# A conditioned feed-forward kernel: the aggregation of its channel mixes taken from TensorE to VectorE and GpSimd

## Chip, core and metric

One Trainium2 (trn2) chip, one core of it. The metric is the device time of one execution in microseconds (us), lower is better. Engines: PE is TensorE, DVE is VectorE, ACT is ScalarE, POOL is GpSimd, SP is SyncE, which here only issues DMAs.

## What is computed

For 64 samples, x is 32 channels by 512 features, and a condition vector of 128 numbers belongs to each sample.

```python
h   = gelu(cond @ W0 + b0); h = gelu(h @ W1 + b1)
att = softmax(h @ W2 + b2)                        # 64 x 8
agg_w = einsum('bk,koi->boi', att, weight)        # a 32 x 32 mix for each sample
agg_b = att @ bias_k                              # 64 x 32
hs    = einsum('boi,bih->boh', agg_w, x) + agg_b[:, :, None]
logits = hs @ gate_w;  r = sum(top_2(logits))
shared = relu(hs @ up_w)**2 @ down_w              # 512 -> 1024 -> 512
routed = ((hs @ fc1_w) @ expert_w * r) @ fc2_w    # 512 -> 256 -> 256 -> 512
out = x + layernorm(shared + routed) * gamma + beta
```

All inputs and the output are float32.

## The kernel before, in words

The 64 samples make 16 tiles of 128 rows (4 samples of 32 channels), and the tiles make 4 blocks of 4. Each large product is done as three products of parts, high times high, high times low and low times high (`three_products`, L773 to L776), where the high part is the value rounded to float32r, which ACT writes with a copy, and the low part is the rest, which DVE writes with a subtraction: `up_hi`/`up_lo` (L416, L542), `h_hi`/`h_lo` (L425, L561), `down_hi`/`down_lo` (L478, L664), `sq_hi`/`sq_lo` (both DVE, L589 and L591).

**Head.** PE computes the small network (L725, L728, L732, L733) between filler products that write a bank nobody reads (`stay_warm`, L714). The softmax is spread over ACT and DVE (L410 to L516). The attention is transposed (L740), split (L520, L522), and multiplied with the split kernel tensor in eight products (L746), which leaves every sample's 32 x 32 mix in a PSUM bank. Sixteen small copies of 32 x 32 (L433 on ACT, L569 on DVE) put block 0's mixes on the diagonal of `mix`; sixteen of 32 x 128 (L446, L586) later put all of them into `agg`, from which POOL builds `mix` for the next blocks (`next_mix`, L366). The bias rows come from a product of ones with split products of attention and bias (L527 to L535, L755). `fold_expert` (L719) makes expert_w times fc2_w in plain float32; of its eight calls two stand in the head, one after the mix products of block 0, and five after the first four up chunks.

**Blocks.** Each block does on PE: mix (L760, `mix_chunk`), up (`up_chunk`, eight column groups of four chunks), latent and gate products, then mix of the next block, then down. In block 0 the up products run chunk by chunk over four column groups at once (`up_first_block`, L783), since h arrives chunk by chunk, and then four groups in turn, each of which waits until ACT has emptied its bank (`relu_done`).

**Orders that matter here.** Every engine works through its instructions in the order written. `late` is one buffer of 16 KB a partition: it first takes the raw up weights, then the raw down weights, then x plus beta (`x_beta`) and the output tiles. So SP issues the down loads (L315) only after all of up has been split (L312, L313). POOL's order is: constants, `fc1_lo` (L351), the low gate part (L354), then for block 0 `x_plus_beta` (L371), which waits until two quarters of down have been split (L381, L382), then `next_mix`. SP loads the next block's x into `x_cur` (L319 to L321) only after `xbeta_ready`, since x_plus_beta reads the old x. PE waits for that load at L903, ahead of the next block's mix products.

ACT's order in block 0 is: relu and square of group 0 and 1, each followed by `q_high` (L420), of groups 2 to 5, each followed by a quarter of `down_high`, then 6 and 7. DVE follows with the same pattern (`split_square`, `q_low`, `down_low`). `relu_square` of group m waits for `sq_lo` of group m-2 (L455).

Of the kernel before, what the change touches and what calls it, by code (L numbers as in the profile page):

```python
# [5 lines left out]
def adaln_ffn_kernel(  # L6
# [37 lines left out]
    SR = kernels.shape[0]  # L44
    FIRST, LAST = slice(0, K), slice(SR - K, SR)
# [11 lines left out]
    ONE_BITS = 0x3F800000  # L57
    GC = 96
    WB = 4
    UPC = INT // 4  # L60
# [7 lines left out]
    MIX0_BANK = [7, 4, 7, 4]  # L68
# [7 lines left out]
    experts_v = experts.rearrange("(k p) n -> p k n", p=P)  # L76
    aggb_dram = nc.dram_tensor("aggb_dram", (NB * C,), fp32).ap()

    ctx = ExitStack()
    with ctx:  # L80
# [3 lines left out]
        def sem(name):  # L84
            return ctx.enter_context(nc.semaphore(name))
# [58 lines left out]
        kernels_sb = sb("kernels_sb", [SR, kernels.shape[1]])  # L144
        weight_raw = kernels_sb[:, 0:C * C]
        bias_raw = kernels_sb[:, C * C:C * C + C]
        b2_sb = kernels_sb[0:1, C * C + C:C * C + C + K]
# [3 lines left out]

        att = relu_sq[0:NB, 0, 0:SR]
        att_T = relu_sq[0:2 * K, 1, 0:NB]

        att_parts = sq_hi[0:SR, C * C // TOK, 0:NB]
        weight_parts = sq_hi[0:SR, 0:C * C // TOK, :].rearrange("k a n -> k (a n)")
        bias_parts = sq_lo[0:2 * K, 0, :]
# [3 lines left out]
        att_bias = y_buf[0:2 * K, 0, 0:TOK]  # L161
# [4 lines left out]
        ones = sq_lo[0:2 * K, 1, 0:P]  # L166
# [6 lines left out]
        LOGIT = ps[0:NB, 4, 192:192 + K]  # L173
        ATT_T = ps[0:SR, 4, 256:256 + NB]
        IDLE = ps[0:GC, 0, 0:2 * GC]
        AGG_B = ps[:, 1, :]
        AGGB_ROWS = ps[0:NB, 3, 0:C]
# [3 lines left out]

        AGG = ps[:, 5, :].rearrange("p (c b) -> p c b", b=NB)

        def agg_src(q, g, tiles):

            return AGG[q * C:(q + 1) * C, :, g:tiles * G:G]

        def agg_part(g, q):
            return agg[g * C:(g + 1) * C, :, q:C:G].rearrange("i n c -> i c n")

        def mix_part(g, q):
            return mix[g * C:(g + 1) * C, :, g * C + q:(g + 1) * C:G].rearrange("i t c -> i c t")
# [13 lines left out]
        kernels_loaded = sem("kernels_loaded")  # L206
        experts_loaded = sem("experts_loaded")
        x_loaded = sem("x_loaded")
        up_loaded = [sem(f"up_loaded{i}") for i in range(4)]
# [19 lines left out]
        att_hi_ready = sem("att_hi_ready")  # L229
        att_lo_ready = sem("att_lo_ready")  # L230
        weight_hi_ready = sem("weight_hi_ready")
        weight_lo_ready = sem("weight_lo_ready")
        attb_hi_ready = sem("attb_hi_ready")
        attb_lo_ready = sem("attb_lo_ready")
        agg_done = sem("agg_done")
# [12 lines left out]
        agg_act = sem("agg_act")  # L248
        agg_dve = sem("agg_dve")
        up_hi_ready = sem("up_hi_ready")  # L250
        up_lo_ready = sem("up_lo_ready")
        fc1_hi_ready = sem("fc1_hi_ready")
# [44 lines left out]
        def _(sp):  # L297
            sp.dma_start(mlp_sb[:, :], mlp).then_inc(mlp_loaded, 16)
            sp.dma_start(kernels_sb[:, :], kernels).then_inc(kernels_loaded, 16)
            sp.dma_start(experts_sb[:, :, :], experts_v).then_inc(experts_loaded, 16)  # L300
            sp.dma_start(x_cur[:, :, :], x_v[:, 0:TB, :]).then_inc(x_loaded, 16)
            for i in range(4):
                sp.dma_start(up_raw[:, :, i * UPC:(i + 1) * UPC],
                             up_v[:, :, i * UPC:(i + 1) * UPC]).then_inc(up_loaded[i], 16)

# [6 lines left out]
            sp.wait_ge(up_hi_ready, 4)  # L312
            sp.wait_ge(up_lo_ready, IC)  # L313
# [28 lines left out]
        def _(pool):  # L342
# [6 lines left out]
            nc.gpsimd.memset(half[:, :], -0.5).then_inc(const_ready, 1)  # L349
            pool.wait_ge(fc1_hi_ready, 1)  # L350
# [5 lines left out]
            pool.wait_ge(agg_act, 2 * G)  # L356
            pool.wait_ge(agg_dve, 2 * G)
# [38 lines left out]
        def _(act):  # L396

            act.wait_ge(dve_const, 1)
# [570 lines left out]
```

## Time and profile before

| | |
|---|---|
| runs of the kernel | 268.87 us median of 3 (268.6 to 269.01) |
| profiled execution, span from the first to the last instruction | 266.2 us |
| busy share of the span | PE 97%, DVE 58%, ACT 32%, POOL 17% |
| instructions | 3377 |

The profile is that of one execution; its own time is not given apart from its span, and the median of the runs is 2.7 us above the span. A row of a timeline or chain gives the start and the duration in us, the engine and the line. A row of a group of instructions gives their count, then their busy time and the mean duration in ns of one, then the idle time of the engine just before them and what ended it. PEld is PE's weight load.

### The profile page before, as it was taken

The page shows a single profiled execution, that of the slowest core. Times are in us where ns is not written, and L with a number is a line of the kernel's source. Part 1 is how long each engine was busy: PE and PEld are TensorE (multiplying, and loading weights), DVE is VectorE, ACT ScalarE, POOL GpSimd, SP SyncE. Part 2 cuts the span into 40 slices and gives each one's busy share as a digit, 9 for nine tenths or more (in the row PEclk, how much of TensorE's full clock was granted, in tenths as well). Part 3 has the DMA queues.
Part 4 walks back from the last instruction along what each step waited for, and adds up shares of the span by engine and source line. Part 5 has one row for each costly group of instructions (what it writes and reads, how often), then busy time and mean ns, then how long its engine had stood idle before and what let it go on. Part 6 is the DMA issues. An engine that isn't in the chain of part 4 may idle for free.

```text
span 266.2 us, 3377 instructions
## 1 busy us (share of the span) xinstructions
PE 259.0 (97%) x1222; PEld 215.7 (81%) x1222; DVE 154.9 (58%) x268; ACT 85.2 (32%) x146; POOL 44.6 (17%) x42
## 2 busy tenths in 40 slices
PE   7999999999999999999999999999999999999991
PEld 7698888788888888888888888888888888778891
DVE  3686899974444954384544963384444963314454
ACT  4356994441111354241110354231110355211110
POOL 1000409101111800001111810001111700001111
PEclk9999999999999999999999999999999999999997
DMA  6973710400111240000111140000111100001111
GB/s 211 342 224 147 264 52 10 151 0 0 42 39 39 49 151 0 0 0 4 39 39 39 42 155 0 0 0 0 39 39 39 42 0 0 0 2 39 39 39 39
DMA packets 9132, 15.71 MB, mean 59 GB/s; under 512 B 634, under 2 KB 3578, under 8 KB 9122
## 3 DMA queue, kind: packets, MB, share of 16 engines
q1 hardware_dynamic: 9122, 15.57, 17.4%
q8 instruction: 7, 0.11, 0.2%
q14 instruction: 3, 0.02, 0.0%
HBM read 11.37 MB, written 4.20 MB: 58 GB/s over the span
## 4 chain that ended last, share of the span: by engine, by line
PE 95%; issue 2%; DVE 1%; POOLq 0%; POOL 0%; DVEq 0%
PE ps L774 26%; PE ps L776 26%; PE ps L775 26%; PE ps L760 6%; PE ps L714 2%; PE ps L719 2%; PE ps L838 1%; PE ps L840 1%; PE ps L746 1%; PE ps L850 1%; POOLq L80 0%; POOL rstd L378 0%; PE ps L755 0%; DVE stats L617 0%; DVE y_buf L615 0%
## 5 line engine op out<-in xcount | busy, mean ns | idle before, releaser
L774 PE MATMUL ps<-down_hi,sq_hi 128*128 128x512 f32 (+1 forms) x136 | 51.3, 377 | 0.0
L775 PE MATMUL ps<-down_lo,sq_hi 128*128 128x512 f32 (+1 forms) x136 | 51.2, 377 | 0.0
L776 PE MATMUL ps<-down_hi,sq_lo 128*128 128x512 f32 (+1 forms) x136 | 51.2, 377 | 0.0
L774 PE MATMUL ps<-h_hi,up_hi 128*128 128x512 f32 x128 | 50.3, 393 | 0.0
L776 PE MATMUL ps<-h_hi,up_lo 128*128 128x512 f32 x128 | 49.8, 389 | 0.0
L775 PE MATMUL ps<-h_lo,up_hi 128*128 128x512 f32 x128 | 49.8, 389 | 0.0
L378 POOL TENSOR_TENSOR rstd<-mv,half 128x1 f32<-128x1 f32 x16 | 15.7, 982 | 177.4 <-DVE mv L622 171.9
L456 ACT ACTIVATE relu_sq<-ps 128x512 f32<-128x512 f32 x32 | 19.1, 597 | 58.1 <-PE ps L776 44.2
L615 DVE TENSOR_TENSOR y_buf<-ps,y_buf 128x512 f32<-128x512 f32 x15 | 10.4, 691 | 45.9 <-PE ps L776 45.9
L589 DVE CAST sq_hi<-relu_sq 128x512 fp32r<-128x512 f32 x32 | 23.6, 737 | 20.9 <-ACT relu_sq L458 20.2
L473 ACT ACTIVATE y_buf<-ps,top 128x512 f32<-128x512 f32 x16 | 11.0, 689 | 69.2 <-PE ps L776 67.2
L591 DVE TENSOR_TENSOR sq_lo<-relu_sq,sq_hi 128x512 fp32r<-128x512 f32 x32 | 31.0, 967 | 1.1
L775 PEld LDWEIGHTS ps<-down_lo,sq_hi 128*128 128x128 f32 x136 | 25.6, 188 | 4.7
L774 PEld LDWEIGHTS ps<-down_hi,sq_hi 128*128 128x128 f32 x136 | 25.6, 188 | 4.7
L776 PEld LDWEIGHTS ps<-down_hi,sq_lo 128*128 128x128 f32 x136 | 25.6, 188 | 4.6
L776 PEld LDWEIGHTS ps<-h_hi,up_lo 128*128 128x128 f32 x128 | 24.0, 188 | 5.0
L775 PEld LDWEIGHTS ps<-h_lo,up_hi 128*128 128x128 f32 x128 | 24.0, 188 | 5.0
L774 PEld LDWEIGHTS ps<-h_hi,up_hi 128*128 128x128 f32 x128 | 24.0, 188 | 5.0
L371 POOL TENSOR_TENSOR late<-x_cur,affine_sb 128x2048 f32<-128x2048 f32 x4 | 18.9, 4714 | 10.5 <-DVE down_lo L664 7.6
L458 ACT ACTIVATE relu_sq<-relu_sq 128x512 f32<-128x512 f32 x32 | 20.2, 632 | 1.0
L760 PE MATMUL ps<-mix,x_cur 128*128 128x128 f32 x128 | 18.0, 297 | 0.0
L760 PEld LDWEIGHTS ps<-mix,x_cur 128*128 128x128 f32 x128 | 16.8, 209 | 1.2 <-DMA x_cur<-in_x_dram 0.3
(105 smaller groups left out, 302.4 us busy)
## 6 DMA issues: line engine op xcount, KB each, us to landing
x_cur<-in_x_dram SPq DMA_DIRECT2D x4, 1024.0 KB, 5.5
out_dram<-late SPq DMA_DIRECT2D x15, 256.0 KB, 2.0
late<-in_up_w_dram SPq DMA_DIRECT2D x4, 512.0 KB, 10.0
late<-in_down_w_dram SPq DMA_DIRECT2D x4, 512.0 KB, 5.3
experts_sb<-in_experts_dram SPq DMA_DIRECT2D x1, 768.0 KB, 5.1
agg_b<-aggb_dram SPq DMA_DIRECT2D x1, 768.0 KB, 8.1
latents_sb<-in_latents_dram SPq DMA_DIRECT2D x1, 528.0 KB, 3.9
affine_sb<-in_affine_dram SPq DMA_DIRECT2D x1, 512.0 KB, 5.4
```

The source lines that it names most:

```text
L371: nc.gpsimd.tensor_tensor(x_beta, x_cur[:, :, :], beta_b.unsqueeze(1).to_broadcast([P, TB, HID]), ALU.add).then_inc(xbeta_ready, 1)
L378: nc.gpsimd.tensor_tensor(rstd[:, :], mv[:, 1:2], half[:, :], ALU.pow).then_inc(rstd_done, 1)
L456: nc.scalar.activation(relu_sq[:, m % 2, :], ps[:, UP_BANK[m], :], ACT.Relu).then_inc(relu_done, 1)
L458: nc.scalar.activation(relu_sq[:, m % 2, :], relu_sq[:, m % 2, :], ACT.Square).then_inc(square_done, 1)
L473: nc.scalar.mul(y_buf[:, t % 2, :], routed(t), top2[:, t:t + 1]).then_inc(scaled_done, 1)
L589: nc.vector.tensor_copy(sq_hi[:, m, :], relu_sq[:, m % 2, :]).then_inc(sq_hi_ready, 1)
L591: nc.vector.tensor_tensor(sq_lo[:, m, :], relu_sq[:, m % 2, :], sq_hi[:, m, :].bitcast(fp32), ALU.subtract).then_inc(sq_lo_ready, 1)
L615: nc.vector.tensor_tensor(y, shared(t), y, ALU.add).then_inc(y_done, 1)
L760: last = nc.tensor.matmul(ps[:, bank, t * P:(t + 1) * P], x_cur[:, t, c * P:(c + 1) * P], mix[:, t, :], start=True, stop=True)
L774: nc.tensor.matmul(dst, a_hi, b_hi, start=first, stop=False)
L775: nc.tensor.matmul(dst, a_hi, b_lo, start=False, stop=False)
L776: return nc.tensor.matmul(dst, a_lo, b_hi, start=False, stop=last)
```

## The change

It replaces the head and touches nothing from the latent product of block 0 on, but for the wait for the old aggregates.

- The kernel tensor is loaded by four DMAs that ACT issues ahead of its first activation (256 pieces of 128 bytes), the bias rows by one small DMA on SP. The up weights come in five DMAs in place of four, the first two half as long.
- DVE repeats the kernel tensor along the columns, PE transposes it in two products, and DVE copies the result to `weight_T`. All this stands ahead of the logits on both engines.
- DVE makes 0/1 selectors from the identity. The attention is spread over the partitions by one product of the selector with `att_tiles`, and stays in PSUM (`ATT_P`).
- The mixes of block 0 are one multiplication and one reduction of 128x1024 on DVE, then four copies of 32x128 to `mix`, two each on ACT and DVE.
- The mixes of blocks 1 to 3 are made on POOL: for each block a multiplication of 128x1024 and three additions of 128x512, 128x256 and 128x128, all on SBUF. They stand ahead of `fc1_lo` in POOL's order.
- POOL also makes the products of attention and bias (8x512) and the low parts of up's column groups 0, 1 and 3. DVE keeps groups 2 and 4 to 7.
- The product of the bias rows is plain float32 in place of one float32r product. The split of attention and kernel tensor, the eight aggregation products and the 32 small copies are gone.
- Of the 26 filler products ahead of the first mix 14 stay (10, 2 and 2). Two `fold_expert` calls move from behind the start of the mix into the head.
- SP waits for `up_lo_pool` too before the down loads.

```diff
@@ block.sync
-            sp.dma_start(kernels_sb[:, :], kernels).then_inc(kernels_loaded, 16)
+            sp.dma_start(bias_sb[:, :], kernels[0:K, C * C:]).then_inc(bias_loaded, 16)
...
-            sp.wait_ge(up_hi_ready, 4)
-            sp.wait_ge(up_lo_ready, IC)
+            sp.wait_ge(up_hi_ready, IC)
+            sp.wait_ge(up_lo_ready, 5)
+            sp.wait_ge(up_lo_pool, 3)
@@ block.gpsimd, ahead of fc1_lo
+            pool.wait_ge(attT_copied, 1)
+            nc.gpsimd.tensor_tensor(
+                att_bias.rearrange("k (b o) -> k b o", o=C),
...
+                ALU.mult).then_inc(attb_ready, 1)
+            for m in (0, 1, 3):
+                cols = slice(m * P, (m + 1) * P)
+                pool.wait_ge(up_hi_ready, [1, 2, 4, 4][m])
+                nc.gpsimd.tensor_tensor(up_lo[:, :, cols], up_raw[:, :, cols], up_hi[:, :, cols].bitcast(fp32),
+                                        ALU.subtract).then_inc(up_lo_pool, 1)
...
+            for j in range(1, NBLK):
...
+                nc.gpsimd.tensor_tensor(
+                    rest_terms,
+                    weight_T[:, :, :].unsqueeze(1).to_broadcast([P, TB, C, K]),
+                    att_P[:, j * TB:(j + 1) * TB, :].unsqueeze(2).to_broadcast([P, TB, C, K]),
+                    ALU.mult).then_inc(rest_terms_ready, 1)
+                pool.wait_ge(rest_terms_ready, 3 * j - 2)
+                nc.gpsimd.tensor_tensor(rest_terms[:, :, :, 0:4], rest_terms[:, :, :, 0:4], rest_terms[:, :, :, 4:8],
+                                        ALU.add).then_inc(rest_terms_ready, 1)
...
+                nc.gpsimd.tensor_tensor(agg[:, j * TB:(j + 1) * TB, :], rest_terms[:, :, :, 0],
+                                        rest_terms[:, :, :, 1], ALU.add).then_inc(rest_agg_ready, 1)
@@ block.scalar
+            for k in range(KH):
+                act.dma_start(weight_raw[k * C:(k + 1) * C, :, :], weight_v[:, :, k, :]).then_inc(weight_loaded, 16)
...
+            act.wait_ge(first_agg_ready, 1)
+            for g in (0, 1):
+                r = slice(g * C, (g + 1) * C)
+                nc.scalar.copy(mix[r, :, r], agg[r, 0:TB, :]).then_inc(mix0_act, 1)
             act.wait_ge(aggb_done, 1)
             nc.scalar.copy(agg_b[:, 0:TOK], AGG_B).then_inc(aggb_copied, 1)
...
+            split_up(0)
             split_up(1)
             mix_high(0, [0])
+            split_up(2)
             mix_high(0, [1, 2, 3])
-            split_up(2)
             split_up(3)
-            for q in (0, 1):
-                for g in range(G):
-                    nc.scalar.copy(agg_part(g, q), agg_src(q, g, NT)).then_inc(agg_act, 1)
+            split_up(4)
@@ block.vector
+            dve.wait_ge(weight_loaded, 16 * KH)
+            nc.vector.tensor_copy(weight_rep[:, :, :, :],
+                                  weight_raw[:, :, :].unsqueeze(2).to_broadcast([P, K // KH, G, C])
+                                  ).then_inc(weight_rep_ready, 1)
+            dve.wait_ge(weightT_done, 1)
+            nc.vector.tensor_copy(weight_T[:, :, :], WEIGHT_T.rearrange("p (k o) -> p o k", o=C)
+                                  ).then_inc(weightT_copied, 1)
...
+            nc.vector.tensor_tensor(
+                first_terms, weight_T[:, :, :].unsqueeze(1).to_broadcast([P, TB, C, K]),
+                ATT_P[:, 0:TB, :].unsqueeze(2).to_broadcast([P, TB, C, K]), ALU.mult).then_inc(first_terms_ready, 1)
+            dve.wait_ge(first_terms_ready, 1)
+            nc.vector.tensor_reduce(agg[:, 0:TB, :], first_terms, AX.X, ALU.add).then_inc(first_agg_ready, 1)
...
             dve.wait_ge(aggb_copied, 1)
             mix_bias(0, 0)
-            split_up(2)
             mix_low(0, 0)
             mix_bias(0, 1)
-            split_up(3)
+            split_up(2)
             mix_low(0, 1)
...
             split_up(4, 2)
             split_up(6, 2)
-            for q in (2, 3):
-                for g in range(G):
-                    nc.vector.tensor_copy(agg_part(g, q), agg_src(q, g, NT)).then_inc(agg_dve, 1)
@@ block.tensor
+            pe.wait_ge(const_ready, 1)
+            pe.wait_ge(weight_rep_ready, 1)
+            for a in range(K // KH):
+                last = nc.tensor.transpose(WEIGHT_T[:, a * P:(a + 1) * P],
+                                           weight_rep[:, a, :, :].rearrange("p g i -> p (g i)"), ident[:, :])
+            last.then_inc(weightT_done, 1)
...
+            nc.tensor.matmul(ATT_P.rearrange("p t k -> p (t k)"), sel[:, :, :].rearrange("b g i -> b (g i)"),
+                             att_tiles[:, :, :].rearrange("b t k -> b (t k)"),
+                             start=True, stop=True).then_inc(attP_done, 1)
...
-            for c in range(C // G):
-                last = nc.tensor.matmul(AGG[:, c, :], weight_parts[:, c * P:(c + 1) * P], att_parts[:, :],
-                                        start=True, stop=True)
-            last.then_inc(agg_done, 1)
...
+            nc.tensor.matmul(AGGB_ROWS, att_T[:, :], bias_raw, start=True, stop=True).then_inc(rows_done, 1)
+            fold_expert(0, 1, 0)
+            fold_expert(0, 1, 1).then_inc(q_done, 1)
+            pe.wait_ge(attb_ready, 1)
+            nc.tensor.matmul(AGG_B, ones[:, :], att_bias, start=True, stop=True).then_inc(aggb_done, 1)
```

## Rows read from the trace of the kernel before

**Rows 1.** The page: span, busy time by engine, and the chain that ended last

```profile
span 266.2 us, 3377 instructions
...
PE 259.0 (97%) x1222; PEld 215.7 (81%) x1222; DVE 154.9 (58%) x268; ACT 85.2 (32%) x146; POOL 44.6 (17%) x42
...
PE 95%; issue 2%; DVE 1%; POOLq 0%; POOL 0%; DVEq 0%
```

**Rows 2.** The chain in order of time, 0 to 20 us (start, us, what)

```profile
6.88 1.14 PE ps L719 x2
...
13.60 4.56 PE ps L760 x24
18.16 0.43 PE ps L719 x2
```

**Rows 3.** Windows, L760 alone (us, busy and records of PE and PEld, granted clock, DMA)

```profile
13.60:16.90 3.30, 3.30 (x15) 3.30 (x16) 1.00 0.49 153
...
51.90:53.60 1.70, 1.70 (x15) 1.70 (x16) 1.00 0.00 0
```

**Rows 4.** Timeline of ACT, 0 to 8 us

```profile
4.04 0.31 ACT L402 ACTIVATE hid<-ps,mlp_sb 128x64 f32<-128x64 f32 x1 [1.80 <-PE ps L725]
...
5.53 1.28 ACT L407 ACT_TABLE_LOAD   x1
...
6.93 0.25 ACT L410 ACTIVATE att_exp<-ps,neg_max 64x8 f32<-64x8 f32 x1
```

**Rows 5.** Who waited for whom, 40 to 60 us (total, times, longest)

```profile
POOL late L371 <- DVE down_lo L664: 7.6, 1, 7.6
...
PEld ps L760 <- DMA x_cur<-in_x_dram: 0.3, 1, 0.3
```

**Rows 6.** Timeline of SP, 26 to 60 us, and line L321's time to landing

```profile
27.11 2.03 SPq L315 DMA_DIRECT2D late<-in_down_w_dram  x4
45.14 0.39 SPq L321 DMA_DIRECT2D x_cur<-in_x_dram  x1
...
DMA to landing us min/median/max: 5.3/5.5/5.5
```

**Rows 7.** Timeline of PE, 50.3 to 52 us

```profile
50.66 1.58 PE L760 MATMUL ps<-mix,x_cur 128*128 128x128 f32 x9
```

**Rows 8.** Timeline of POOL, 29.8 to 50.9 us

```profile
29.87 2.37 POOL L351 TENSOR_TENSOR fc_lo<-latents_sb,fc_hi 128x1024 fp32r<-128x1024 f32 x1 [27.88 <-ACT fc_hi L448]
...
40.28 4.63 POOL L371 TENSOR_TENSOR late<-x_cur,affine_sb 128x2048 f32<-128x2048 f32 x1 [7.64 <-DVE down_lo L664]
```

**Rows 9.** Timeline of DVE beside them

```profile
31.22 1.31 DVE L589 CAST sq_hi<-relu_sq 128x512 fp32r<-128x512 f32 x1 [0.75 <-ACT relu_sq L458]
...
38.81 1.22 DVE L664 TENSOR_TENSOR down_lo<-late,down_hi 128x1024 fp32r<-128x1024 f32 x1
39.95 0.42 DVE L589 CAST sq_hi<-relu_sq 128x512 fp32r<-128x512 f32 x1
40.40 5.07 DVE L591 TENSOR_TENSOR sq_lo<-relu_sq,sq_hi 128x512 fp32r<-128x512 f32 x1
```

**Rows 10.** Groups of POOL's instructions, 0 to 52 us

```profile
L366 POOL COPY mix<-agg 32x128 f32<-32x128 f32 x4 | 2.8, 692 | 0.3
...
L348 POOL MEMSET mix<- 128x512 f32 x1 | 0.5, 525 | 0.0
```

**Rows 11.** Groups of DVE's instructions, 0 to 52 us

```profile
L586 DVE COPY agg<-ps 32x128 f32<-32x128 f32 x8 | 3.2, 400 | 0.2
L561 DVE TENSOR_TENSOR h_lo<-h_full,h_hi 128x512 fp32r<-128x512 f32 x4 | 2.8, 692 | 1.6 <-ACT h_hi L425 1.4
L556 DVE TENSOR_TENSOR h_full<-ps,agg_b 128x512 f32<-128x512 f32 x4 | 2.7, 687 | 0.5 <-PE ps L760 0.5
```

**Rows 12.** Groups of ACT's instructions, 0 to 52 us

```profile
L416 ACT CAST up_hi<-late 128x1024 fp32r<-128x1024 f32 x4 | 4.1, 1048 | 0.0
...
L425 ACT CAST h_hi<-h_full 128x512 fp32r<-128x512 f32 x4 | 2.5, 622 | 5.1 <-DVE h_full L556 5.1
```

More of the change, by code:

```diff
@@ L41, in adaln_ffn_kernel @@
     K = mlp.shape[1] - NB - 2 * D - 2
-    SR = kernels.shape[0]
-    FIRST, LAST = slice(0, K), slice(SR - K, SR)
+    KH = 4
     INT = up_w.shape[1]
@@ L143, in adaln_ffn_kernel @@
         b1_sb = mlp_sb[:, NB + 2 * D + K + 1:NB + 2 * D + K + 2]
[L144 to L147, printed above, removed]
+        weight_raw = sb("weight_raw", [P, K // KH, C])
+        weight_rep = sb("weight_rep", [P, K // KH, G, C])
+        weight_T = sb("weight_T", [P, C, K])
+        bias_sb = sb("bias_sb", [K, C + K])
+        bias_raw = bias_sb[:, 0:C]
+        b2_sb = bias_sb[0:1, C:C + K]
+        sel_g = sb("sel_g", [NB, G])
+        sel = sb("sel", [NB, G, C])
+        in_tile = sb("in_tile", [NB, NT])
+        att_tiles = sb("att_tiles", [NB, NT, K])
+        att_P = sb("att_P", [P, NT, K])
         hid1 = sb("hid1", [D, NB])
@@ L150, in adaln_ffn_kernel @@
         att_exp = sb("att_exp", [NB, K])
[L152 to L157, printed above, removed]
+        att = sb("att", [NB, K])
+        att_T = sb("att_T", [K, NB])
+        first_terms = relu_sq[:, :, :].rearrange("p a (t o k) -> p (a t) o k", o=C, k=K)
+        rest_terms = y_buf[:, :, :].rearrange("p a (t o k) -> p (a t) o k", o=C, k=K)
         neg_max = sb("neg_max", [NB, 1])
@@ L165, in adaln_ffn_kernel @@
         logits = sb("logits", [P, TB, NE])
-        ones = sq_lo[0:2 * K, 1, 0:P]
+        ones = sb("ones", [K, P])
         half = sb("half", [P, 1])
@@ L205, in adaln_ffn_kernel @@
         mlp_loaded = sem("mlp_loaded")
-        kernels_loaded = sem("kernels_loaded")
+        weight_loaded = sem("weight_loaded")
+        bias_loaded = sem("bias_loaded")
         experts_loaded = sem("experts_loaded")
         x_loaded = sem("x_loaded")
-        up_loaded = [sem(f"up_loaded{i}") for i in range(4)]
+        up_loaded = [sem(f"up_loaded{i}") for i in range(len(UP_COLS))]
         latents_loaded = sem("latents_loaded")
@@ L565, in _ @@
             dve.wait_ge(const_ready, 2)
-            dve.wait_ge(agg_done, 1)
-            for q in (2, 3):
-                for g in range(G):
-                    nc.vector.tensor_copy(mix_part(g, q), agg_src(q, g, TB)).then_inc(mix0_dve, 1)
-            split_up(0, 2)
+            dve.wait_ge(first_agg_ready, 1)
+            for g in (2, 3):
+                r = slice(g * C, (g + 1) * C)
+                nc.vector.tensor_copy(mix[r, :, r], agg[r, 0:TB, :]).then_inc(mix0_dve, 1)
             dve.wait_ge(aggb_copied, 1)
             mix_bias(0, 0)
-            split_up(2)
             mix_low(0, 0)
             mix_bias(0, 1)
-            split_up(3)
+            split_up(2)
             mix_low(0, 1)
@@ L583, in _ @@
             split_up(6, 2)
-            for q in (2, 3):
-                for g in range(G):
-                    nc.vector.tensor_copy(agg_part(g, q), agg_src(q, g, NT)).then_inc(agg_dve, 1)
             def split_square(b, m):
@@ L770, in _ @@
             mix_chunk(0, 2, MIX0_BANK[2])
-            fold_expert(0, 1, 0)
             def three_products(dst, a_hi, a_lo, b_hi, b_lo, first, last):
@@ L798, in up_first_block @@
                         mix_chunk(0, 3, MIX0_BANK[3])
-                fold_expert(0, 1, 1).then_inc(q_done, 1)
-                pe.wait_ge(h_ready, 3)
                 for half in (0, 1):
```

172 lines of the change are left out of this document (85 added, 87 removed).

## The prediction

> **What bounds the kernel now.** I read the page first: PE is busy for 97% of the span and holds 95% of the chain that ended last [rows 1]. So the kernel is PE's list of products, and a change counts where it moves PE's start, shortens the list or makes PE wait. Next came the chain in order of time: the mix products start at 13.60, the last `fold_expert` call ahead of the up products at 18.16 [rows 2], and from there on the chain holds no wait to speak of. Then I looked for places where PE has no reserve. There is one at 50.66, block 1's first mix products [rows 7]: the weight load in front of them was released by the load of x [rows 5]. That load comes out of a chain beside PE: two quarters of down split on DVE, for which POOL waited 7.6 us [rows 5], `x_plus_beta` on POOL from 40.28 to 44.91 [rows 8], the DMA issued at 45.14 and 5.5 us to its landing [rows 6], 50.6. This chain is as long as PE's own work, to 0.1 us. Whatever delays it, PE waits for.
>
> Last I looked at DVE beside POOL. While POOL subtracted 128x1024 (29.87 to 32.24) a DVE cast of 0.42 took 1.31, and while `x_plus_beta` ran, a DVE subtraction that takes 0.69 otherwise took 5.07 and ended at 45.47, 0.55 after POOL's end [rows 8, 9]. So the two exclude one another for the whole instruction. The addition of PSUM and SBUF (L556) shows no such mean, nor does L561, which ran when POOL was idle [rows 11].
>
> **The head.** The four DMAs that ACT now issues cost about 0.45 each (SP's one x issue takes 0.39, [rows 6]), 1.8 us ahead of its first table load; ACT had 1.80 us idle before the first gelu [rows 4], so I take nothing for them. When they land is not shown: at 4.3 they delay nothing, as the exponential is held by ACT's own table load (5.53 to 6.81, [rows 4]); at worst I take the 5.5 of the x load from the last issue, 7.6, which puts repeat, transposition, logits and exponential 2 us later. I take 4.3, since the pieces are few and small, and keep 2 us for the range. Three fewer fillers ahead of the second layer give back 0.15.
>
> DVE then has a multiplication and a reduction of 1024 elements, 1.2 each by the 128x1024 subtraction [rows 9], from 8.8 (behind the fold and the spread) to 11.2, and four copies in two pairs of 0.4 each [rows 11]: mixes ready at 12.1. PE is later. A fold call takes 1.14 in the head and 0.43 at 18.16 [rows 2]. The mix products tell why: 15 records in 3.30 us from 13.6, 15 in 1.70 later [rows 3], half the pace for one shape, though the granted clock stands at 1.00 (2.4 GHz) in both: the first stretch goes at the pace of 1.2 GHz, until PE had run them for 3.3 us on end. From 8.0 on, the end of the first fold, PE has the spread and the transposition 0.7, three folds 3.4, the bias rows 0.3, and the bias product, now plain float32 with twice a fold's columns: two fold calls less one pair of weight loads, 2.0 (as one float32r product of the same columns it needed a quarter of the passes). All slow that is 14.5; if the pace doubles at once, 12.1, where DVE bounds. PE is now dense from 6.9 on, so I let it double inside the bias product: mix at **14.0** against 13.60. The Trainium skill, TensorE: Matmul & The Clock Gate, Part 1, says that the array starts slow and that sustained activity releases it; by that rule alone the pace would double well before the bias product and the mixes would start near 12.1, 1.9 us earlier than I take.
>
> The first chunk then takes eight records at 0.11 [rows 3] and 0.3 to its reader, 1.2; bias, high and low part take 0.69, 0.62 and 0.69 [rows 11, 12]: PE starts the up products near 17.3, where the chain before had 18.6 [rows 2]. POOL's rate is 4634/2048 = 2.26 ns an element of the row [rows 8], so 1.2 for one `up_lo` of 512. POOL starts the first at 15.3 (bias product to 14.1, ACT's copy of it 0.6, half an up quarter on ACT 0.55, [rows 12]) and alternates with two subtractions of DVE (0.69 each): 15.3 + 3 x 1.24 + 1.4 = **20.4** when POOL is through with up. PE loses some 0.8 on column groups 1 and 3, which wait for POOL, and one of the two moved folds (0.43) is off its list behind this point. Taken alone, that is a gain of about 1 us.
>
> **The aggregates on POOL.** This is the term that decides. From 20.4 POOL has 3 x (1024 + 512 + 256 + 128) = 5760 elements, then `fc1_lo` and the gate, 1056: 6816 x 2.26 ns = 15.4 us. In the same stretch DVE must do, with both inputs in SBUF, three `h_lo` (0.69 each), two `up_lo` of 1024 and two `down_lo` (1.22 each), the split of squares 0 to 3 (0.42 and 0.69) and one cast more, 0.4 [rows 9, 11]: 11.8 us. By [rows 8, 9] none of this overlaps, whichever goes first, but for the hand-over: the 5.07 ended 0.55 behind POOL, 0.14 less than its 0.69. Some ten of those are worth 1.4, and POOL's pauses between dependent instructions eat part of it; I take off 0.6. `x_plus_beta` starts at 20.4 + 15.4 + 11.8 - 0.6 = **47.0**, where it started at 40.28. It ends 4.63 later, SP issues 0.2 later, and x lands 5.5 later: **57.3**. PE, at 50.66 before, goes on at 57.35: **+6.7 us**. The down loads start when DVE is through with up, near 31 instead of 27.11 [rows 6], and are in time for this. The squares come late too (the last ones behind `x_plus_beta`), so PE stands partly at the gate products and partly at the mix; both lie inside the 6.7. DVE's copies of `agg` (3.2 us, [rows 11]) and as many on ACT are gone, but they held neither side's share of the ports as POOL does now, and are not in the sum.
>
> The Trainium skill, SBUF — State Buffer, Who interferes with whom, says that a VectorE instruction with two SBUF inputs, or in a two-port mode, and a GpSimd one that reads SBUF block each other for the whole instruction, and one with at most one SBUF input does not. By that rule the bias additions, the reduction and the first multiplication, whose second input is in PSUM, are free, and the rest adds up as above. The trace agrees, with 5.07 and 1.31.
>
> POOL's rate on these short rows is not shown. Below: a memset of 512 took 0.53 [rows 10], 1.03 ns an element; 5760 of them save 7.1 us, all of the loss. Above: a copy of 128 took 0.69 with DVE beside it [rows 10], 5.4 ns; for the 2688 elements of the additions 8.4 us more. I take 2.26, the same kind of instruction and type.
>
> After the mix of block 1 nothing differs. Sum: 266.2 + 6.7 = 272.9 of span. The median of the runs is 2.67 above the span, so 275.6. A measurement here can tell about 0.2%, 0.54 us, from no change.
>
> **Rivals.**
> - POOL and DVE overlap, or POOL is twice as quick: then POOL is free at 38 and the down parts decide, two at 38 rather than 40.03, since ACT and DVE lose 3.2 us of `agg` copies each [rows 11]. x lands near 48.5 and PE's own list bounds, 1.0 us earlier: **267.9**. It decides once `x_plus_beta` starts before 40. For it: DVE was idle enough before. Against: the 5.07. Chance 0.14.
> - They exclude each other, but POOL goes at some 1.6 ns an element: 3.8 us less, **271.8**. 0.14. Near enough to nothing (POOL almost at the memset's rate) 0.06.
> - The pace of PE stays low until about 17, or the kernel tensor lands late: mix at 14.6 to 16, and all behind it moves with it, POOL's start too: **277.7**, up to 280. 0.10.
> - The clock rule's case, mix at 12.1 with POOL's queue still in the way: POOL is through with up at 17.5 to 18.5, x lands near 55: **273.6**. It is inside the main case's range. Main case with it: 0.56.
>
> **Numbers.** Likeliest is the main case, 275.6, with 273 to 278 of its own. Faster has only the first rival, 0.14; same 0.06; slower 0.80. Leaving those two out, the range starts at 269.5 and takes in the slow head, 280.5.
>
> **What would show it.** Right: POOL busy without a pause from about 15 to 52; DVE's `sq_lo`, `sq_hi` and `h_lo` in block 0 with means far above 0.7; `x_plus_beta` starting at 45 to 49; PE idle several us before L760 of block 1, released by x, and before gate or latent by ACT. Wrong: `x_plus_beta` starting by 41, DVE's durations unchanged beside POOL's multiplications, the mix starting outside 12 to 14.6, or a wait of several us ahead of the first up product.

## The result and the profile after

The changed kernel takes 277.35 us, the median of four runs (276.59 to 278.39), the kernel before beside it 268.74 (268.33 to 269.01): 1.030 times as long, interval 1.026 to 1.035. The profiled execution is the fastest of the four, 276.59, with a span of 274.8 against 266.2 [rows 1]: 8.6 us more. One slow run of the kernel before (908.4 us, beside e9 to e11) and the longest of e3 below are left out of the ratios, the first of its median too.

The page: span, busy time, chain.

```profile
span 274.8 us, 3346 instructions
...
PE 260.0 (95%) x1207; PEld 213.2 (78%) x1207; DVE 158.3 (58%) x251; ACT 82.3 (30%) x136; POOL 67.5 (25%) x58
...
PE 78%; DVE 10%; DMA 4%; issue 3%; POOL 2%; ACT 1%; ACTq 0%; POOLq 0%; DVEq 0%; SPq 0%
```

PE is as busy as before, 260.0 us against 259.0, but holds 78% of the chain in place of 95%: the added time is waiting, and POOL has gone from 44.6 to 67.5 us. Where PE waits is seen best at the same product as in [rows 7], block 1's first mix product. PE's timeline, 50 to 61 us:

```profile
52.81 0.39 PE L809 MATMUL ps<-h_hi,fc_lo 128*128 128x512 f32 x1
54.86 0.44 PE L875 MATMUL ps<-h_hi,gate_hl 128*96 128x512 f32 x1 [1.67 <-ACT relu_sq L496]
...
59.24 2.01 PE L794 MATMUL ps<-mix,x_cur 128*128 128x128 f32 x13 [2.32 <-DMA x_cur<-in_x_dram]
```

59.24 against 50.66 is 8.6 us, as much as the spans differ: all of the loss stands ahead of this point. 4.0 of it is waiting in these rows (1.67 and 2.32). The rest is older, and the chain in order of time tells its beginning (start, us, what; 0 to 24 us), where [rows 2] had PE at 6.88 and the mix at 13.60:

```profile
2.15 5.46 DMA weight_raw<-in_kernels_dram
7.60 0.02 issue
7.63 0.30 DVE weight_rep L553
...
15.15 2.00 PE ps L790 x2
17.15 2.02 PE ps L794 x8
```

The chain now begins with the four small loads of the kernel tensor. The waits of 0 to 14 us (total, times, longest) say who stood for them:

```profile
DVE weight_rep L553 <- DMA weight_raw<-in_kernels_dram: 5.6, 1, 5.6
PE ps L767 <- DVE weight_rep L553: 2.9, 1, 2.9
...
ACT att_exp L444 <- DVE neg_max L561: 2.6, 1, 2.6
```

Everything waits until 7.6, so the exponential runs at 9.64 where [rows 4] had 6.93, and the mix begins at 17.08. Windows of the mix products alone (columns as in [rows 3]):

```profile
17.08:20.87 3.79, 3.79 (x17) 3.79 (x18) 1.00 0.89 357
20.87:21.65 0.78, 0.78 (x8) 0.78 (x7) 1.00 0.00 0
```

0.22 us each until 20.87, then 0.10: the same change of pace as in [rows 3], 3.8 us after the mix began. The loads end at about the same time (their share falls from 0.89 to 0.00), but it is not they that hold PE back: in the kernel before 9 records took the 1.35 us from 15.40 at a DMA share of 0.07, and in e7, an experiment below, the pace doubles from 8 records to 14 in 1.35 us at 15.10, with the share at 1.10 on both sides. Last POOL, its timeline from 18 us on:

```profile
18.50 2.51 POOL L360 TENSOR_TENSOR up_lo<-late,up_hi 128x512 fp32r<-128x512 f32 x2 [5.42 <-ACT up_hi L460]
...
22.89 2.83 POOL L369 TENSOR_TENSOR y_buf<-weight_T,att_P 128x1024 f32<-128x1024 f32 x1
...
31.53 1.61 POOL L375 TENSOR_TENSOR y_buf<-y_buf 128x512 f32<-128x512 f32 x1
33.22 1.48 POOL L378 TENSOR_TENSOR y_buf<-y_buf 128x256 f32<-128x256 f32 x1
...
41.86 2.40 POOL L384 TENSOR_TENSOR fc_lo<-latents_sb,fc_hi 128x1024 fp32r<-128x1024 f32 x1
...
48.87 4.61 POOL L403 TENSOR_TENSOR late<-x_cur,affine_sb 128x2048 f32<-128x2048 f32 x1 [4.21 <-DVE down_lo L699]
```

and DVE beside it:

```profile
23.40 2.87 DVE L601 TENSOR_TENSOR h_lo<-h_full,h_hi 128x512 fp32r<-128x512 f32 x1
26.19 0.68 DVE L596 TENSOR_TENSOR h_full<-ps,agg_b 128x512 f32<-128x512 f32 x1
...
31.92 3.87 DVE L582 TENSOR_TENSOR up_lo<-late,up_hi 128x1024 fp32r<-128x1024 f32 x2
...
42.12 2.43 DVE L624 CAST sq_hi<-relu_sq 128x512 fp32r<-128x512 f32 x1
```

`h_lo`, 0.69 in [rows 11], takes 2.87 beside the multiplication of 2.83; a cast of 0.42 takes 2.43 beside `fc1_lo`. The addition with one input in PSUM (`h_full`) keeps its 0.68. The end of this is SP's queue, behind [rows 6] by 8.8 and 8.6 us:

```profile
35.86 1.92 SPq L315 DMA_DIRECT2D late<-in_down_w_dram  x4
53.70 0.39 SPq L321 DMA_DIRECT2D x_cur<-in_x_dram  x1
```

### The profile page after: what moved, and what is told of

Same layout as the page of the kernel before. It is cut to its first block, busy times and chain, and to the rows that moved or that the text cites. A ratio compares the mean times of both kernels' runs of the same rounds, so it can differ in the third digit from the quotient of the medians.

```text
span 274.8 us, 3346 instructions
## 1 busy us (share of the span) xinstructions
PE 260.0 (95%) x1207; PEld 213.2 (78%) x1207; DVE 158.3 (58%) x251; ACT 82.3 (30%) x136; POOL 67.5 (25%) x58
## 3 DMA queue, kind: packets, MB, share of 16 engines
q1 hardware_dynamic: 9616, 15.40, 16.1%
## 4 chain that ended last, share of the span: by engine, by line
PE 78%; DVE 10%; DMA 4%; issue 3%; POOL 2%; ACT 1%; ACTq 0%; POOLq 0%; DVEq 0%; SPq 0%
PE ps L807 22%; PE ps L808 22%; PE ps L809 22%; PE ps L794 5%; DMA x_cur<-in_x_dram 2%; DMA weight_raw<-in_kernels_dram 2%; DVE sq_lo L626 2%; DVE up_lo L582 2%; POOL late L403 2%; DVE sq_hi L624 2%; PE ps L754 1%; DVE h_lo L601 1%; PE ps L875 1%; PE ps L877 1%; DVE h_full L596 1%
## 5 line engine op out<-in xcount | busy, mean ns | idle before, releaser
L624 DVE CAST sq_hi<-relu_sq 128x512 fp32r<-128x512 f32 x32 | 25.4, 793 | 20.2 <-ACT relu_sq L498 19.7
L650 DVE TENSOR_TENSOR y_buf<-ps,y_buf 128x512 f32<-128x512 f32 x15 | 10.4, 692 | 46.2 <-PE ps L809 46.2
L626 DVE TENSOR_TENSOR sq_lo<-relu_sq,sq_hi 128x512 fp32r<-128x512 f32 x32 | 33.3, 1040 | 1.1
```

What stands on the lines that cost most here:

```text
L624: nc.vector.tensor_copy(sq_hi[:, m, :], relu_sq[:, m % 2, :]).then_inc(sq_hi_ready, 1)
L626: nc.vector.tensor_tensor(sq_lo[:, m, :], relu_sq[:, m % 2, :], sq_hi[:, m, :].bitcast(fp32), ALU.subtract).then_inc(sq_lo_ready, 1)
L650: nc.vector.tensor_tensor(y, shared(t), y, ALU.add).then_inc(y_done, 1)
```

## Experiments

The theory to test: the loss has two terms that add up, a head 3 us late for the weight loads (the loads of the kernel tensor), and aggregates on POOL that take DVE's ports and so delay `x_plus_beta` and the load of x. "Ports" stands here for whatever the two engines keep each other out of in [rows 8, 9]. The rivals: that the head is hidden behind the rest, that POOL's own time and not its ports is what costs, or that something else in the head does it. The edits of e1 to e6, e8 and e10 are to the changed kernel, that of e7 is to e6, and those of e9 and e11 are to e7. The kernel before, run beside them, had medians of 269.68, 269.79 and 269.95 on the chips used, against 268.74 above, so each kernel is read by its profile and its ratio too. Its runs there lie between 267.44 and 270.98, and their granted clocks do not sort them (269.64 at 0.974, 267.62 at 0.980, 270.79 at 0.995). Why they spread stays open.

### Weight loads earlier (e1)

```diff
@@ block.sync, behind mlp
+            for k in range(2, KH):
+                sp.dma_start(weight_raw[k * C:(k + 1) * C, :, :], weight_v[:, :, k, :]).then_inc(weight_loaded, 16)
@@ block.scalar
-            for k in range(KH):
+            for k in range(2):
```

> The changed kernel, with two of the four loads of the kernel tensor issued by SP, right behind the first load, and two by ACT (SP's later loads start 0.9 us later). In the changed kernel the four landed at 3.1, 3.5, 5.6 and 7.6 us, and weight_rep waited for the last. Theory (the head is late since the last two queued behind the big loads): all land by 5, the first mix starts near 14.4 rather than 17.1, x_plus_beta and the x load move with it by 2.7, time 274.6 +- 0.7. Rival (the experts load, 0.9 later, takes over, as fold_expert stands ahead of the spread product on PE): the mix starts at 15.3 to 16, time 275.6 to 276.5. Rival (block 1's x load doesn't depend on the head): the time stays at 277.

Measured: 275.48 us (273.91 to 275.61, four runs), ratio 1.019 (1.013 to 1.025). The mix starts at 14.39 in place of 17.08, `x_plus_beta` at 46.17 in place of 48.87: 2.7 us at both places, so the head was not hidden. The time is just above the theory's 275.3, but its rival with a mix at 15.3 or later did not come. The span fell by 1.2 only, from 274.8 to 273.6. The 1.5 that are missing stand behind the wait for x. Windows of its profile (us; busy and records of PE, PEld, DVE, ACT, POOL; granted clock; DMA):

```profile
56.00:58.00 2.00, 1.42 (x10) 1.23 (x11) 1.97 (x5) 0.50 (x2) 0.00 (x0) 1.00 0.03 8
58.00:60.00 2.00, 2.00 (x12) 2.00 (x12) 1.44 (x3) 0.62 (x1) 0.00 (x0) 0.56 0.01 4
60.00:62.00 2.00, 2.00 (x13) 1.74 (x12) 0.36 (x2) 0.62 (x1) 0.00 (x0) 0.59 0.00 0
```

The same place in the changed kernel's profile:

```profile
60.00:62.00 2.00, 1.97 (x18) 1.78 (x17) 1.95 (x4) 0.40 (x1) 0.00 (x0) 1.00 0.04 12
```

After PE had stood idle twice (1.6 us ahead of the gate products, 1.9 ahead of the mix), the granted clock fell to about the lower level, 1.2 GHz, for some 3.5 us, and 12 or 13 products were done in a window of 2 us in place of 18. One of the four runs, 273.91, has a mean granted clock of 0.998, the other three 0.987 to 0.990; that run has all the 2.7 us. The changed kernel's own four runs are split the same way: 276.59 and 276.90 at 0.998, 277.79 and 278.39 at 0.990 and 0.987. The length of the waits alone does not decide it: the changed kernel's profiled execution kept its clock behind 1.67 and 2.32.

The edit moves two loads to another queue and ahead of the big loads at once. Which of the two brought the 2.7 us is not separated.

### No aggregates on POOL (e2), and both (e5)

```diff
@@ block.gpsimd
-            for j in range(1, NBLK):
...
+            nc.gpsimd.memset(agg[:, TB:NT, :], 0.0).then_inc(rest_agg_ready, NBLK - 1)
```

> The changed kernel without the aggregates of blocks 1 to 3: POOL sets them to zero with one memset in their place, so the mixes of those blocks are left out. Theory (POOL's 19 us of aggregates, each excluding DVE's two-input subtractions, delay x_plus_beta and with it the x load): h_lo, up_lo and the squares on DVE are back at 0.69, 1.22 and 0.42, the down loads start near 28 rather than 35.9, x_plus_beta near 42 rather than 48.9, and PE no longer waits for x; its list then puts block 1's mix at 54.0 rather than 59.2: 272.0 +- 0.8. Rival (the loss is the late head alone): the time stays above 276.

Measured: 271.13 us (270.88 to 271.48, ten runs), ratio 1.005 (1.002 to 1.008); 6.2 us less, and as the theory had it but for 0.1. POOL's timeline in its profile:

```profile
42.90 4.62 POOL L387 TENSOR_TENSOR late<-x_cur,affine_sb 128x2048 f32<-128x2048 f32 x1 [9.19 <-DVE down_lo L683]
```

and DVE's:

```profile
23.75 0.68 DVE L585 TENSOR_TENSOR h_lo<-h_full,h_hi 128x512 fp32r<-128x512 f32 x1
...
28.87 2.36 DVE L566 TENSOR_TENSOR up_lo<-late,up_hi 128x1024 fp32r<-128x1024 f32 x2 [0.33 <-ACT up_hi L444]
33.90 0.43 DVE L608 CAST sq_hi<-relu_sq 128x512 fp32r<-128x512 f32 x1 [2.67 <-ACT relu_sq L482]
```

DVE's durations are those of [rows 9, 11] again, and `x_plus_beta` starts 6.0 us earlier, although the mix began at 17.45, no earlier than in the changed kernel. No wait of PE is left between 14 and 62 us.

> Both at once: two of the four loads of the kernel tensor on SP, and POOL's aggregates of blocks 1 to 3 left out (zeros, so the mixes of those blocks are left out). Theory (the two causes add, once PE's list bounds again): 271.1 less the 2.7 us by which the head came earlier, 268.4 +- 0.7, and PE waits neither for x nor for a relu. Rival (with the head early, the chain of down, x_plus_beta and the x load binds as in the kernel before): PE waits for x at block 1's mix and the time is 269.5 or more.

Measured for e1 and e2 in one kernel: 268.25 us (268.14 to 268.58, ten runs), ratio 0.998 (0.995 to 1.001), a span of 266.4, as the theory had it. In spans: e2 takes off 5.3, e1 2.7 at the full clock (its run of 273.91), e5 8.4. The two terms add up to within 0.4, and with both gone all but 0.2 of the loss of 8.6 is gone.

### A busy POOL without reads (e3)

```diff
@@ block.gpsimd
+            for j in range(15):
+                pool.wait_ge(rest_terms_ready, j + 1)
+                nc.gpsimd.memset(y_buf[:, :, :], 0.0).then_inc(rest_terms_ready, 1)
```

> As before, but POOL fills the place of the aggregates with 15 memsets of 1024 elements, about 16.5 us, which read nothing; the mixes of blocks 1 to 3 are left out. Theory (ports): DVE's subtractions with two SBUF inputs are undisturbed beside POOL's memsets, the casts at most a little; x_plus_beta starts near 42.5, when POOL gets to it, and the time is within 1 us of that of the kernel without the aggregates, 272 to 273. Rival (it is POOL's queue alone, not what it does to DVE): DVE's rows are no shorter than with the aggregates, and x_plus_beta moves by no more than the 2.5 us by which POOL's stretch is shorter, to 46 or later: 274.5 or more.

Measured: 273.57 us (270.96 to 275.38, ten runs), ratio 1.015 (1.010 to 1.019). `x_plus_beta` starts at 46.10, and not near 42.5 as the theory had it: by this number the rival came out, which had 46 or later. The rows of the two engines tell the two apart. POOL's timeline:

```profile
23.86 15.46 POOL L369 MEMSET y_buf<- 128x1024 f32 x15
39.44 0.20 POOL L371 MEMSET half<- 128x1 f32 x1
39.49 2.41 POOL L373 TENSOR_TENSOR fc_lo<-latents_sb,fc_hi 128x1024 fp32r<-128x1024 f32 x1
```

DVE's beside it:

```profile
28.02 0.69 DVE L590 TENSOR_TENSOR h_lo<-h_full,h_hi 128x512 fp32r<-128x512 f32 x1 [0.69 <-ACT h_hi L458]
29.04 2.36 DVE L571 TENSOR_TENSOR up_lo<-late,up_hi 128x1024 fp32r<-128x1024 f32 x2 [0.33 <-ACT up_hi L449]
34.07 1.17 DVE L613 CAST sq_hi<-relu_sq 128x512 fp32r<-128x512 f32 x1 [2.66 <-ACT relu_sq L487]
...
38.66 0.94 DVE L613 CAST sq_hi<-relu_sq 128x512 fp32r<-128x512 f32 x1
39.63 2.82 DVE L615 TENSOR_TENSOR sq_lo<-relu_sq,sq_hi 128x512 fp32r<-128x512 f32 x1
```

Memsets leave DVE's subtractions alone (0.69, and 2.36 for two of 1024): 15.5 us of a busy POOL cost them nothing, so for them the reads on POOL decide and not POOL's time. But each of three casts, 0.42 otherwise, waits for a memset (1.17, 0.94 and 0.94, 1.8 us in all), and `fc1_lo`, 8.8 us later than in e2 (30.74), now meets a `sq_lo` (2.82 in place of 0.69, 2.1 us). That is 3.9, of which DVE's pauses in e2 (0.28 and 0.47) take up 0.75: the 3.2 us between 42.90 and 46.10. So 3.2 of the 6.0 us that e2 gained at `x_plus_beta` are lost again, and the 2.8 that are left come with a stretch on POOL that is 3 us shorter (16.0 against 19.0). The exclusion is shown by the durations; how much of the 6.0 it is by itself, this run does not separate.

The ten runs fall into three groups: two at 270.96 and 271.16, which is e2's time, five from 273.23 to 273.76, and three from 274.83 to 275.38. The profiled execution is the longest; its granted clock fell behind a single wait for x of 1.65 us, to 0.52 in the window from 58, which lies behind all the rows above. What the two short runs did differently is not shown.

The Trainium skill, SBUF — State Buffer, Who interferes with whom, says that a VectorE instruction with two SBUF inputs collides with a GpSimd one that reads SBUF but not with one that only writes it, and that casts in a two-port mode collide with either. The rows agree: 0.69 against 1.17.

### The aggregates of blocks 2 and 3 later (e4)

```diff
@@ block.gpsimd
-            for j in range(1, NBLK):
+            rest(1, rest_terms)
@@ pool_block(0), behind next_mix(0)
+                    for j in range(2, NBLK):
+                        rest(j, late_terms)
```

`rest` is the body of the loop, and `late_terms` lies in `latents_sb`, which is free by then.

> The changed kernel, complete, with the aggregates of blocks 2 and 3 made behind x_plus_beta and next_mix of block 0 (in the dead raw latent tile) and only block 1's ahead. Theory (ports and order): POOL's stretch ahead of x_plus_beta falls by 13 us, that starts at 42 to 44, PE waits for x by less than 1 us: 272.5 +- 1. Rival (the two aggregates collide with DVE's work at the block's end, where h_lo of block 1 is due, and PE waits there instead): 274 to 277.

Measured: 276.58 us (276.33 to 277.69, four runs), ratio 1.026 (1.020 to 1.032), 0.8 less only, and the spans are the same, 274.8. `x_plus_beta` came 5.2 us earlier, at 43.63, and x landed at 54.4. But PE then stood from 55.8 to 58.9. Its waits, 14 to 62 us:

```profile
PE ps L803 <- DVE lat_lo L641: 3.1, 1, 3.1
```

POOL's timeline:

```profile
51.47 3.26 POOL L371 TENSOR_TENSOR latents_sb<-weight_T,att_P 128x1024 f32<-128x1024 f32 x1
54.81 1.33 POOL L377 TENSOR_TENSOR latents_sb<-latents_sb 128x512 f32<-128x512 f32 x1
```

DVE's:

```profile
52.39 2.62 DVE L633 CAST sq_hi<-relu_sq 128x512 fp32r<-128x512 f32 x1
55.05 1.64 DVE L635 TENSOR_TENSOR sq_lo<-relu_sq,sq_hi 128x512 fp32r<-128x512 f32 x1
```

The theory's 271.5 to 273.5 failed, and the rival came out: the aggregates collide with DVE's last squares of block 0 and hold up the latent split behind them, and the granted clock fell again (0.68 and 0.50 in the windows from 58 and 60). Late is not enough; it must be a place where DVE has nothing urgent.

### Spread over the blocks (e6), with the folds back (e7)

e6 is e1 with block 1's aggregate where it was, and those of blocks 2 and 3 at the start of POOL's part for blocks 1 and 2, whose loop is written out. e7 also puts the two `fold_expert` calls back behind the start of the mix. Both compute everything.

```diff
@@ e6, block.gpsimd
-            with pool.Fori(1, NBLK - 1) as b:
-                pool_block(b)
+            for b in range(1, NBLK - 1):
+                rest(b + 1, late_terms)
+                pool.wait_ge(rest_agg_ready, b + 1)
+                pool_block(b)
@@ e7, block.tensor
-            fold_expert(0, 1, 0)
-            fold_expert(0, 1, 1).then_inc(q_done, 1)
...
             mix_chunk(0, 2, MIX0_BANK[2])
+            fold_expert(0, 1, 0)
```

> Complete: loads early, and the aggregates spread: block 1's ahead of fc1_lo as in the change, block 2's behind the inverse deviations of block 0, block 3's behind those of block 1. Theory: x_plus_beta of block 0 starts near 41, x lands by 52, the last squares are not disturbed as they were when both stood behind next_mix, and PE's list bounds, with 1 to 1.6 us lost beside the first chunks, where POOL's block 1 stands against h_lo: 269.9 +- 0.8. Rival (the aggregates cost wherever they stand, since DVE's squares open the next block): 272 or more, with PE waits in blocks 1 and 2.

> The kernel before this one, with two fold_expert calls back behind the start of the mix. Theory (in the head they run at half the pace and stand in front of the bias product): the first mix comes 1.9 us earlier, near 12.5, the list behind it is 0.86 longer, 1.0 us less in all: 268.9 +- 0.8. Rival (POOL's and ACT's splits of up hold the first up products, not the mix): the same time as without the edit, within 0.4, with PE idle behind the mix.

Measured: e6 268.80 us (267.7 to 268.88, ten runs), ratio 0.998 (0.995 to 1.001); e7 267.33 (267.27 to 267.52, ten runs), ratio 0.993 (0.990 to 0.996). e6 came out under its range of 269.1 to 270.7: PE lost less beside the first chunks than expected, and waits nowhere over 0.3 us between 14 and 62. It has `x_plus_beta` at 40.73 against 39.74 in e5: the 5.8 us of POOL's work for block 1 cost 1.0 where they stand. e7 gave 1.5 where 1.0 was expected, and so lies under its range too. PE's timeline of e7:

```profile
10.42 2.07 PE L797 MATMUL ps<-y_buf,ones 8*128 8x512 f32 x2
12.42 4.29 PE L801 MATMUL ps<-mix,x_cur 128*128 128x128 f32 x24
16.54 0.60 PE L763 MATMUL ps<-experts_sb 128*128 128x256 f32 x2
```

and POOL's:

```profile
38.91 4.64 POOL L410 TENSOR_TENSOR late<-x_cur,affine_sb 128x2048 f32<-128x2048 f32 x1 [7.61 <-DVE down_lo L708]
```

Ahead of the mix, two records of a fold take 1.1 to 1.2 at the low pace; at 16.54 they take 0.60, and PE has time there while DVE adds the bias. e7 is under both kernels: 10 us under the change by medians of two sessions, and 2.5 under the kernel before by the medians of one chip. That last gain is small, 0.7% with the interval clear of 1, and the spans of the two profiled executions differ by 0.7 us only (265.5 and 266.2).

### Block 1's aggregate behind the gate split (e11)

```diff
@@ block.gpsimd, e7
-            rest(1, rest_terms)
             pool.wait_ge(fc1_hi_ready, 1)
...
+            rest(1, rest_terms)
             pool.wait_ge(rest_agg_ready, 1)
```

> The kernel with early loads, spread aggregates and the folds back (267.3 us), with block 1's aggregate moved behind fc1_lo and the low gate part. Theory (the place decides: it leaves h_lo and up_lo alone, worth 0.5 us, but stands against the squares and down_lo on which x_plus_beta waits): x_plus_beta starts 2 to 3.5 us later, at 41 to 42.5 rather than 38.9, x lands at 51 to 52.5 against PE's need near 49.5, and the time is 268.3 to 270. Rival (DVE's squares have reserve, the chain has 0.8 us or more): 266.8 to 267.3.

Measured: 268.49 us (268.25 to 268.84, five runs), ratio 0.994 (0.991 to 0.997). As the theory had it: `x_plus_beta` starts at 40.73 in place of e7's 38.91, and PE waits 0.3 for x. The same work on POOL puts `x_plus_beta` 1.8 us later at 29 than at 18, where DVE has waits of 0.7 for ACT between chunks, and the median 1.2 us higher.

### The low parts of up back on DVE (e8), and in the best kernel (e9)

```diff
@@ block.gpsimd
-            for m in (0, 1, 3):
...
@@ block.vector
             dve.wait_ge(aggb_copied, 1)
+            split_up(0)
             mix_bias(0, 0)
+            split_up(1)
...
             split_up(2)
+            split_up(3)
```

> The changed kernel with the low parts of up's column groups 0, 1 and 3 back on DVE, nothing else. Theory (ports): POOL starts its aggregates near 17.3 rather than 22.9, DVE gets 2.1 us more to do, x_plus_beta starts some 3 to 4 us earlier, near 45.5, and the first up products some 1 us later: 273.5 to 275. Rival (DVE is what is short here, so taking work from POOL back to it costs): 277.4 or more.

> The kernel with early loads, spread aggregates and the folds back (267.3 us), with the low parts of up's groups 0, 1 and 3 back on DVE. With all aggregates ahead of x_plus_beta this edit gave 2.1 us, while PE lost 3.1 beside the first chunk to DVE's late up_lo. Theory (with the chain through x no longer binding, only the loss is left, since POOL's block 1 now stands right against DVE's up_lo): 268.8 to 270. Rival (POOL's aggregate is over earlier and gives it back): 267.3 or less.

Measured: e8 275.28 us (275.17 to 276.48, four runs), ratio 1.026 (1.021 to 1.032), 2.1 less and just above the theory. POOL's aggregates start at 17.58 in place of 22.89, 5.3 earlier, yet `x_plus_beta` at 47.58 is only 1.3 earlier, where the theory had 3 to 4: they run beside the up splits that moved to DVE, as DVE's timeline shows.

```profile
23.71 4.45 DVE L575 TENSOR_TENSOR up_lo<-late,up_hi 128x512 fp32r<-128x512 f32 x2
```

PE then waits for those (2.3 us in two waits) but no more for x, and the granted clock stays at 1.00. e9, this edit in e7, took 267.77 us (267.48 to 267.95, four runs), ratio 0.990 (0.987 to 0.993). The theory had a loss of 1.5 us or more against e7, and 0.4 was measured in another session, with ratios whose intervals overlap: the size was wrong, and which of the two is faster stays open.

### PE kept busy ahead of the wait for x (e10)

```diff
@@ block.tensor
+                    if first_block:
+                        pe.wait_ge(relu_done, IC)
+                        for i in range(26):
+                            nc.tensor.matmul(ps[0:GC, 3, 0:2 * GC], gate_hl[:, 0, :], gate_hl[:, 1:3, :],
+                                             start=True, stop=True)
                     pe.wait_ge(x_loaded, 16 * (b + 2))
```

> The changed kernel, complete, with 26 filler products (192 columns, 0.08 us each at the full pace) in front of the wait for block 1's x, behind the last relu of block 0. The changed kernel's four runs lie at 276.6 and 276.9 with a mean granted clock of 0.998, and at 277.8 and 278.4 with 0.990 and 0.987. Theory (PE's two idle stretches of 2.1 and 2.7 us ahead of block 1's mix let the granted clock fall in some runs, and the mix products then go at half the pace): the waits stay as they are, no run falls behind them, and all runs lie at 276.6 +- 0.4. Rival (the spread has another cause, or the first idle stretch, ahead of the gate products, is enough): runs of 277.8 and above with clocks of 0.990 and below remain.

Measured: 276.99 us (276.58 to 277.02, four runs), ratio 1.024 (1.021 to 1.027), mean granted clocks 0.995 to 0.998, where two of the changed kernel's four runs were at 277.79 and 278.39. The windows of its profile:

```profile
58.00:60.00 2.00, 2.00 (x25) 2.00 (x24) 1.93 (x4) 1.53 (x4) 0.00 (x0) 1.00 0.21 76
60.00:62.00 2.00, 2.00 (x20) 2.00 (x20) 1.94 (x5) 0.05 (x1) 0.00 (x0) 1.00 0.00 0
```

The fillers take 2.57 us, from 57.51 to 60.08, and x landed near 59.5 (issued at 54.05, 5.4 to landing): so they end behind it and cost some 0.35, as the mix starts 10.72 behind `x_plus_beta` where the changed kernel had 10.37. No run lost its clock. This fits the theory that the idle time lowers the clock, but four runs on each side are few: if half of all runs lose it, as in the changed kernel, four without a loss come by chance once in sixteen.

## Why the prediction was right, and where it was not

**Right.** The direction, the range and the mechanism: that POOL and DVE exclude one another decides, and the loss reaches PE through `x_plus_beta`, SP's load and the first mix products of block 1. From the start of `x_plus_beta` to PE's next product it said 10.3, and 59.24 is 10.4 behind 48.87. That nothing differs behind that point is right too (8.6 there, 8.6 in all), and e2 removes the term: 6.0 us at `x_plus_beta`.

**Right in sum by luck: POOL and DVE as one list.** From POOL's end with up to the start of `x_plus_beta` the prediction said 15.4 + 11.8 - 0.6 = 26.6 us, and 22.89 to 48.87 is 26.0. Two of its terms were off and cancelled. POOL's own work is longer than 15.4: the shortest durations that any run shows (multiplication 2.36 in e9, additions 1.27, 0.61 and 0.42 in e4, `fc1_lo` and the gate 2.37 in [rows 8] and 0.25 in e2) add up to 16.6, and with eleven pauses of 0.08 between them to some 17.5. DVE's 11.8 is right to its parts. So about 3.3 us must have overlapped and not 0.6, an estimate from these rows. The exclusion itself is plain: `h_lo` ended 0.55 behind the multiplication beside it, as the 5.07 had done.

**Mis-sized: the weight loads.** "I take 4.3, since the pieces are few and small". They landed at 3.13, 3.53, 5.65 and 7.60, just its worst value. e1 prices that at 2.7 us, at the mix and at `x_plus_beta`.

**Wrong: the pace inside the bias product.** "I let it double inside the bias product." It doubled at 20.87, 3.8 us into the mix. The all-slow value of the text, 14.5 (its terms add up to 14.4), is what e1 shows once the loads are early: 14.39. Together the two put the mix at 17.08, not 14.0. The kernel before could have told: PE is busy there for all of 1.49 to 13.60, and its pace still doubled only at 16.9, so being dense from 6.9 on was no reason. By the Trainium skill, TensorE: Matmul & The Clock Gate, Part 1, sustained activity releases the clock; taken alone it put the mix at 12.1. The trace differs. Windows of the changed kernel ahead of the mix (columns as for e1):

```profile
11.58:17.08 5.50, 5.50 (x11) 2.45 (x10) 2.88 (x4) 1.14 (x5) 1.04 (x1) 1.00 1.06 322
9.00:11.50 2.50, 2.50 (x10) 1.58 (x9) 0.84 (x4) 0.65 (x3) 0.00 (x0) 1.00 1.13 331
```

PE was busy for all of both, and its folds and bias product stayed at the low pace to their end, two records of each in 1.1 and 2.0 us. The up products came 4.6 us behind the mix, not 3.3, since the first eight mix products took 2.02 and not 0.9.

**The sum.** The 3.1 us of the head reached POOL's end with up as 2.5 (22.89 for 20.4), since POOL began 3.2 late (18.50 for 15.3) but was through in 4.4 rather than 5.1; less the 0.6 by which the port sum was too long, that is 1.9 at `x_plus_beta` (48.87 for 47.0) and in the span (274.8 for 272.9). The profiled execution lies 1.8 above its span, not 2.67, which takes off 0.9, and two of four runs lost clock, which puts the median 0.8 above the profiled one: 277.35 for 275.6. The drop of the clock during PE's waits was no part of the prediction.

**The rival that came true as well.** "The pace of PE stays low until about 17, or the kernel tensor lands late", 277.7, had 0.10. Both halves happened, on top of the main case, and the measured 277.35 lies nearer to this rival's time than to 275.6. 0.10 was too little: the text had the worst landing from a row, 5.5 for a load beside others, and chose the better one by the size of its pieces alone. The rival of overlap (267.9) is excluded by 2.87 for `h_lo`. The quicker POOL (1.6 ns an element) is excluded too: a multiplication of 1024 takes 2.4, 2.35 ns, and an addition of 512 takes 1.6, 3.1 ns, beside DVE, and 1.27, 2.5 ns, at best (e4).

**Its signs.** Means far above 0.7 on DVE, PE released by x and ahead of the gate by ACT: as it said. `x_plus_beta` within 45 to 49: yes. One of its signs of being wrong came too, a mix outside 12 to 14.6: it started at 17.08, so the account of the head is refuted by the text's own measure, though the time lies in the range. Not so: POOL busy without a pause. It stood 5.4 us ahead of `up_lo` for ACT and 4.2 ahead of `x_plus_beta`, while DVE worked off what POOL had held up. The down loads came at 35.86, not near 31: 2.7 of it is the head (33.17 in e1), the rest `h_lo` and `up_lo` held up in turn. In the changed kernel that cost nothing, as DVE came to its first `down_lo` only at 45.2; once the aggregates are spread, the split of down on ACT behind those loads becomes what `x_plus_beta` waits for last (e6: 7.5 us; in e7 it is `down_lo` on DVE again).

## What to carry to other kernels

Work that is moved to an idle GpSimd is not free if VectorE works with two SBUF inputs beside it: count both engines' such instructions as one list (a bound from above: here some 29 us of them took 26.0), and put the moved work where VectorE waits for something else. The same aggregate put `x_plus_beta` 1.0 us later at one place and 1.8 more some 11 us on, and two of them cost 3 us of TensorE's time behind `next_mix`. Ahead of a kernel's first long chain, see what the first small load is queued beside, and don't move TensorE's work into the stretch that runs at the low pace: two folds back out of it gave 1.5 us.

## What the runs showed of the hardware that was not expected

- TensorE's granted clock fell from 1.00 to 0.5 or 0.6 for some 3.5 us after it had stood for 1.6 and 1.9 us (e1), once for 1.65 (e3) or once for 3.1 (e4), in part of the runs only; behind 1.67 and 2.32 in the change's profile it did not fall. It costs 1.3 to 1.6 us a run (the change: 276.7 against 278.1; e1: 273.91 against 275.5).
- Two of four loads in 128-byte pieces issued at 1.67 and 2.15 us, while SP put loads of 0.75 and 1 MB into its queue, landed at 5.65 and 7.60; the two issued first at 3.13 and 3.53.
- A GpSimd memset, which reads nothing, left VectorE's two-input subtractions at 0.69, but made each cast beside it last 0.94 to 1.17 in place of 0.42 (e3).
- Plain float32 products and their weight loads ran 5.5 us on end (11.58 to 17.08) without leaving the low pace, though the granted clock stands at 1.00 in their windows. In the kernel before TensorE was busy from 1.49 on and doubled its pace at 16.9.
